# A slot list's compares, products and row normalisation are dealt out anew between VectorE, GpSimd and ScalarE

## The reference

```python
def _moe_forward(x, gate_w, wg, wu, wd):            # E = 8 experts, I = 512, K = 2
    x_flat = x.reshape(-1, h)
    logits = x_flat @ gate_w.T
    top_v, top_i = jax.lax.top_k(logits, K)
    probs = jax.nn.softmax(top_v.astype(jnp.float32), axis=-1).astype(logits.dtype)
    one_hot = jax.nn.one_hot(top_i, E, dtype=probs.dtype)
    combine = jnp.einsum('tk,tke->et', probs, one_hot)
    def body(acc, ws):
        wge, wue, wde, we = ws
        hidden = jax.nn.silu(x_flat @ wge.T) * (x_flat @ wue.T)
        return (acc + we[:, None] * (hidden @ wde.T), None)
...
x = L0_attn_x
x = x + 0.5 * _L0_ffn_ref(_layernorm(x, axis=-1), gate_w, wg, wu, wd)
x = x + _L0_attn_ref(_layernorm(x, axis=-1), ...)      # two mamba layers, one on the flipped sequence
x = x + 0.5 * _L0_ffn_ref(_layernorm(x, axis=-1), gate_w, wg, wu, wd)
```

## Time and profile before

| what | before |
|---|---|
| time, median of 3 runs | 2839.34 us (2837.99 to 2840.05) |
| the profiled execution: its own time, its span | 2840.15 us, 2838.0 us |
| first routing: normalised rows and logits up to the end of `choose(3)` | up to 51.49 us |
| first routing: the 16 batches, from the first `is_col` to VectorE's start on the lists | 62.22 to 104.96 us |
| second routing: end of `choose(3)`; the 16 batches | 2262.69 us; 2273.44 to 2316.2 us |
| busy shares over the span | PE 81%, DVE 81%, POOL 78%, ACT 67% |

### The profile page before, as it was taken

The page is one execution under the profiler, slowest core; times in us unless marked ns, Lnnn a source line. Parts: engine busy times, 40 slices in busy tenths (PEclk is TensorE's granted clock), DMA queues, the critical chain, the costliest instruction groups (busy, mean ns, idle before and its releaser), DMA issues.

```text
span 2838.0 us, 49251 instructions
## 1 busy us (share of the span) xinstructions
PE 2304.0 (81%) x15924; PEld 1961.5 (69%) x15924; DVE 2287.4 (81%) x3442; ACT 1909.5 (67%) x3640; POOL 2212.1 (78%) x1410
## 2 busy tenths in 40 slices
PE   4888888867887888988888888889897678888883
PEld 3778788835766766777676767677776467778772
DVE  8755555579999999999999999999999775555556
ACT  3344444448978979899999999999988434444441
POOL 3666666628989989999999999999999556666662
PEclk8999999988999999999999999999999889999996
DMA  7011111143333333333333333333333401111116
GB/s 229 20 40 41 40 41 41 39 142 94 103 96 96 101 93 104 104 101 111 102 109 106 108 106 103 106 106 104 110 103 109 160 12 41 41 40 41 40 40 192
DMA packets 155518, 249.13 MB, mean 88 GB/s; under 512 B 22194, under 2 KB 64082, under 8 KB 154578
## 3 DMA queue, kind: packets, MB, share of 16 engines
q1 hardware_dynamic: 136450, 202.92, 23.8%
q0 software_dynamic: 18464, 37.79, 5.0%
q10 hardware_dynamic: 432, 6.29, 0.6%
HBM read 213.36 MB, written 33.55 MB: 87 GB/s over the span
## 4 chain that ended last, share of the span: by engine, by line
PE 42%; DVE 16%; issue 15%; POOL 11%; ACT 10%; DMA 3%; another core or an unknown queue 3%; ACTq 0%; SPq 0%; POOLq 0%; DVEq 0%
PE bank L1339 13%; PE bank L1360 9%; POOL buf L544 8%; PE bank L1535 6%; DVE buf L909 5%; PE bank L1410 4%; PE bank L1510 3%; ACT over L1154 3%; PE bank L1320 3%; DVE X L796 2%; ACT scaled L1187 2%; DMA buf<-state_rows 2%; DVE buf L896 2%; POOL buf L531 2%
## 5 line engine op out<-in xcount | busy, mean ns | idle before, releaser
L544 POOL TENSOR_TENSOR buf<-buf 128x1024 f32<-128x1024 f32 x512 | 1200.6, 2380 | 68.3 <-PE bank L1535 40.1
L909 DVE TENSOR_TENSOR_SCAN buf<-over,bank 128x512 f32<-128x512 f32 x832 | 953.7, 1200 | 8.3 <-ACT over L1154 5.4
L1339 PE MATMUL bank<-parts 128*128 128x256 f32 x3456 | 530.3, 299 | 76.4 <-issue 73.7
L1154 ACT ACTIVATE over<-wgu,negA 128x510 f32<-128x510 f32 x832 | 541.4, 710 | 60.7 <-DVE buf L909 59.7
L1339 PEld LDWEIGHTS bank<-parts 128*128 128x128 f32 x3456 | 460.8, 198 | 96.9 <-issue 91.8
L1535 PE MATMUL bank<-id_sb,buf 128*128 128x128 f32 x4096 | 514.5, 279 | 6.7 <-POOL buf L544 6.7
L1535 PEld LDWEIGHTS bank<-id_sb,buf 128*128 128x128 f32 x4096 | 477.3, 144 | 57.0 <-issue 46.0
L493 POOL DMA_INDIRECT token_outputs<-buf,slot_out x288 | 298.3, 1036 | 266.8 <-ACT buf L1055 199.2
L768 DVE TENSOR_TENSOR buf<-buf,bank 128x512 f32<-128x512 f32 x288 | 196.8, 684 | 332.2 <-ACT buf L1049 204.1
L1187 ACT ACTIVATE scaled<-wd_sb,I 128x256 f32<-128x256 f32 x896 | 377.3, 497 | 22.0 <-PE bank L1510 21.9
L483 POOL DMA_INDIRECT buf<-token_rows,slot_token x288 | 298.9, 1038 | 96.7 <-issue 90.7
(11 more groups left out here) (169 smaller groups left out, 3003.7 us busy)
## 6 DMA issues: line engine op xcount, KB each, us to landing
buf<-state_rows SPq DMA_DIRECT2D x608, 256.0 KB, 3.3
token_rows<-buf SPq DMA_DIRECT2D x32, 256.0 KB, 2.3
wd_sb<-token_outputs SPq DMA_DIRECT2D x16, 512.0 KB, 4.5
buf<-token_outputs SPq DMA_DIRECT2D x16, 512.0 KB, 4.8
buf<-token_rows,slot_token POOLq DMA_INDIRECT x288
token_outputs<-buf,slot_out POOLq DMA_INDIRECT x288
out<-X SPq DMA_DIRECT2D x16, 256.0 KB, 3.6
wgu<-wgT ACTq DMA_DIRECT2D x1, 2048.0 KB, 8.3
```

The lines of the kernel that those rows point to most:

```text
L544: pool.tensor_tensor(hC[:, b, :].rearrange("p (c w) -> p c w", c=C), hs[:, b, :].rearrange("p (c w) -> p c w", c=C), Cs[:, b, :].unsqueeze ...
L909: V.tensor_tensor_scan(hs[:, b, w], dA[:, b, c, :, :].rearrange("p s t -> p (s t)"), source, 0.0, ALU.mult, ALU.add).then_inc(s[f"scan_don ...
L1154: ins = A.activation(dA[:, n % R, c, :, 1:], delta[r][:, c * W:(c + 1) * W].rearrange("p (s t) -> p s t", s=S)[:, :, 1:], ACT.Exp, scale=n ...
L1339: ins = M.matmul(bk[:, c * TP:(c + 1) * TP], w[:, b, cols], xx[:, b, :], start=(j == 0), stop=(j == 2))
```

## The change

Three numbers move, and one new piece of work is written for ScalarE.

- `ACT_TILES` is 3: ScalarE normalises three tiles of each group, VectorE one.
- `POOL_B` is 5: GpSimd multiplies five columns of a batch, ScalarE three.
- `PART_B` is 6: VectorE compares six of the eight partitions of a batch. ScalarE makes the other two as relu(1 - |lane - partition|): an `Abs` for each column with the partition as a bias, and, behind a wait for the two, one `Relu` over both. `hot_act` is therefore counted up twice in a batch, once behind the three products and once behind the `Relu`.
- VectorE copies the row of numbers from PSUM to SBUF once in each routing (`lanes`), since ScalarE reads it from there.

```diff
-ACT_TILES = 2
+ACT_TILES = 3
...
-        COLS, NB, POOL_B = TILES * HT, 8, 6
+        COLS, NB, POOL_B, PART_B = TILES * HT, 8, 5, 6
...
+        lanes = carve(10896, P)
...
                 def constants():
                     dve.wait_ge(s["iota_done"], m + 1)
+                    chain(V.tensor_copy(lanes, iota[:, 0:P]))
...
-                chain(V.tensor_copy(part_of, SLp))
+                chain(V.tensor_copy(part_of, SLp), "parts_known", m + 1)
...
-                    wait(dve, s["hot_act"], m * NBATCH + k - 1)
+                    wait(dve, s["hot_act"], 2 * (m * NBATCH + k - 1))
...
-                    V.tensor_tensor(hot_part[:, k % 2, :, :], iota[:, 0:P].unsqueeze(1).broadcast_to([P, NB, P]),
-                                    part_of[:, js].unsqueeze(2).broadcast_to([P, NB, P]),
+                    mine = slice(k * NB, k * NB + PART_B)
+                    V.tensor_tensor(hot_part[:, k % 2, 0:PART_B, :],
+                                    iota[:, 0:P].unsqueeze(1).broadcast_to([P, PART_B, P]),
+                                    part_of[:, mine].unsqueeze(2).broadcast_to([P, PART_B, P]),
                                     ALU.is_equal).then_inc(s["hot_part"], 1)
...
                     ins.then_inc(s["hot_act"], 1)
+                    act.wait_ge(s["parts_known"], m + 1)
+                    for j in range(PART_B, NB):
+                        at = k * NB + j
+                        ins = A.activation(hot_part[:, k % 2, j, :], lanes, ACT.Abs, scale=-1.0,
+                                           bias=part_of[:, at:at + 1])
+                    ins.then_inc(s["hot_apart"], 1)
+                    act.wait_ge(s["hot_apart"], m * NBATCH + k + 1)
+                    A.activation(hot_part[:, k % 2, PART_B:, :], hot_part[:, k % 2, PART_B:, :], ACT.Relu, scale=-1.0,
+                                 bias=1.0).then_inc(s["hot_act"], 1)
...
-                    pe.wait_ge(s["hot_act"], m * NBATCH + k + 1)
+                    pe.wait_ge(s["hot_act"], 2 * (m * NBATCH + k + 1))
```

More of the change, by code:

```diff
@@ L306, in macaron_kernel @@
             hot_pe hot_part is_col hot_pool hot_act ids_ready
-            gate_spread shift_all_done xn_act lT_pe lT_act lback_pe stats_done dve_norm act_norm xt_pre rstd_done xn_done moment before_done xt_done xnT_done
+            gate_spread shift_all_done xn_act lT_pe lT_act lback_pe stats_done dve_norm act_norm xt_pre rstd_done xn_done moment parts_known hot_apart before_done xt_done xnT_done
             logit_done logits_act route_dve route_pe route_act xin0 xin1 xin2
```

## The result

The changed kernel takes 2846.23 us (median of 8 runs, 2843.63 to 2849.77), the kernel before 2839.89 in the same comparison (2837.99 to 2841.57). The ratio is 1.002, with a 95% interval of 1.001 to 1.0029: slower by 6.3 us, with 2.8 to 8.2 us inside the interval. The forecast was 2843.0, with a range of 2837.5 to 2849.

The account below looks back on a forecast made before the run. VectorE was taken as the limit in both stretches, ScalarE 1.0 and 0.6 us ahead at the logits, TensorE close behind in the batches. Tiles +7.4 and batches -3.7 took 2839.34 to 2843.0 us, range 2837.5 to 2849.

Parts of the forecast that it names:

- the count of 12 tiles: Normalising part: extra ScalarE tiles of groups 4 to 15, 0.39 us each, 4.6 us ahead of quarter 2's logits copy.
- The sum: Both routings: +7.4 us from the tiles and -3.7 from the batches make +3.7 us.
- the loop: Batches: ScalarE and TensorE wait for each other over two batches, 4.40 us a turn, 2.20 a batch instead of 2.40.
- the two hand-overs: Batches: the passing between ScalarE and TensorE in one turn of the loop, taken as 0.11 us.
- the floor: Batches: VectorE's own pace with 256 fewer elements to compare, 2.14 us a batch.
- 0.75 us that is lost beside the steady batches: Ahead of the steady batches: TensorE starts 0.36 us later and batch 2 is filled 0.4 later, in each routing.
- The dear case: Rival: ScalarE's batch instructions cost more, the loop is 2.34 us, in all +8.0 us, 2847.3; chance 0.14.
- The cheap case: Rival: ScalarE's batch chain is 1.84 us, VectorE's 2.14 stays the pace, in all +1.6 us, 2840.9; chance 0.14.
- the logits are not on the path: Rival at `choose(2)`: the third tile delays logits by less than VectorE's lead, -5.9 us, 2833.4; chance 0.07.
- A clock that falls in the logits part: Rival: TensorE's spaced-out matmuls there drop to half clock, +19 us and more, 2862; chance 0.04.
- the forecast's own narrow range: Whole kernel: 2840 to 2846 us, from 0.36 to 0.41 us a tile and batch parts each a little off.

Follow-up runs that it names:

- e1: The kernel before with ACT_TILES = 3 and nothing else of the change: 2689.2 us against 2682.06, ratio 1.0026.
- e4: The changed kernel again without an edit, for a second trace: 2688.91 us against 2682.06 for the kernel before, ratio 1.002.
- e9: The changed kernel with added TensorE matmuls whose results nobody reads, ahead of logits and batches: 2842.2 us against 2840.41 for the kernel before, ratio 1.0005.
- the first trace: The profiled execution of the changed kernel without an edit, from the first comparison; its own time is 2846.79 us.
- e2: The changed kernel with ACT_TILES back at 2, the batches' part alone: 2682.67 us against 2682.06 for the kernel before, ratio 1.0001.
- e3: As e2, with ScalarE's third product back on GpSimd (POOL_B 6): 2679.52 us against 2682.06 for the kernel before, ratio 0.9989.
- e5: As e2, with a third buffer for hot_part and hot_col: 2672.68 us against 2679.83 for the kernel before, ratio 0.9972.
- e8: The kernel before again without an edit, one execution for a second trace; its own time is 2677.25 us.
- e10: The kernel before with a third tile on ScalarE in groups 0 to 3 only: 2841.73 us against 2840.41, ratio 1.0003.
- e11: As e6, with three compares on ScalarE and five on VectorE: 2833.04 us against 2840.41 for the kernel before, ratio 0.9977.
- e6: As e3, with three buffers for hot_part and hot_col: 2670.05 us against 2679.83 for the kernel before, ratio 0.9967.
- e7: The kernel before with three buffers for hot_part and hot_col and nothing of the change: 2675.96 us against 2679.83, ratio 0.9988.

## Why the prediction was right, point by point

**The tiles.** Right in place, mechanism and nearly in size. In the first routing the four traces with the third tile in every group end the last `choose` 3.2 (e1), 3.3 (e4, e9) and 4.2 us (the first trace) after the kernel before; 3.5 was forecast. In the second routing, counted from the constants that VectorE makes behind the `lanes` copy to the last `choose`, so that the projection ahead is left out, all nine traces without the tiles in the late groups have 37.2 or 37.3 us (before, e2, e3, e5 to e8, e10, e11) and the four with them 40.2 to 41.2: +3.0 to +3.9, forecast 3.9. e1 shows that this alone makes the change slower, e10 that the count of 12 tiles was right. The sum had taken TensorE's clock as in the trace of before; where it rises later, the term is 0.9 us larger. The wait ahead of `choose(0)`, which the forecast lacked, is harmless: VectorE waits again, and longer, ahead of `choose(2)`.

**The batches.** The step that was off is the loop: "One turn of that loop is 2.09 + 2.20 + 0.11 for the two hand-overs = 4.40 us". ScalarE's chain is 2.06, so that term was right, `Abs` at 386 ns and `Relu` at 417 with it:

```profile
L1033 ACT ACTIVATE buf<-buf x64: 384/386/388, 68.7 to 2320.1; 128x128 f32<-128x128 f32 x64
...
L1037 ACT ACTIVATE buf<-buf x32: 416/417/417, 69.4 to 2320.5; 128x256 f32<-128x256 f32 x32
```

TensorE's 2.20 was right as well. What was too small is the last term, 0.11 for the two hand-overs: they take 0.14 and 0.10 (the rows at 101.03 to 103.46 above). So the turn is 4.49 us and not 4.40. 13 steady batches gain 13 x 0.15 = 1.95 instead of 2.6, and the 16 together 1.2 in the first trace (0.5 to 1.3 in all six sets of e2, e4 and the first trace). The two sets that gain only 0.5 are those in which TensorE's granted clock comes back 9.4 us behind the first `is_col`; in the other four it is 7.5 to 8.3. e3, e5 and e6 show that the loop is the cause: a shorter chain or a third buffer brings most batches to VectorE's 2.13, which the forecast gave as the floor. e9 shows what the wait for the slow batch 0 costs ahead of the steady ones: 2.0 us of the 41.6. The kernel before has this wait too, and the forecast counted 0.75 us that is lost beside the steady batches; the traces have 0.8, as 0.4 up to batch 2's `hot_part` (7.8 instead of 7.4 us) and 0.4 behind the last `hot_part`, where the lists wait 4.6 instead of 4.2 us.

By the price list of the Trainium skill ("ScalarE: Activation LUTs", section "What ACT_TABLE_LOAD costs") the estimates are 386 ns for the `Abs` and 399 for the `Relu`. The first agrees with the measured 386; the `Relu` takes 417, and there the measurement decides.

**`lanes`.** Taken for hidden. In the first routing e2, e3, e5, e6 and e11 end their last `choose` 0.3 to 0.5 us after the kernel before, and in the second it stands on VectorE's path with its 0.3 in every trace that has it. Whether it is hidden in the changed kernel's first routing no run separates: e4, with it, ends 0.1 us after e1, without it, and the clock rises at different times in the two.

**The second routing's other 1.5 us.** Of the 5.8 us that it lost in the first trace, 3.9 is the tiles. The other 1.8 lies between the last gate and VectorE's constants, 9.8 us instead of 8.0; 0.3 of it is the `lanes` copy. TensorE's first 8 matmuls behind the last gate, and the window around them (columns as under e9, the granted clock is the third from the end), before:

```profile
2218.25 1.09 PE L1435 MATMUL bank<-id_sb,buf 128*128 128x128 f32 x8 [1.38 <-DVE buf L869]
```

```profile
2217.00:2219.00 2.00, 0.75 (x7) 0.75 (x8) 1.91 (x5) 0.06 (x1) 1.91 (x6) 1.00 0.00 0
```

and in the changed kernel:

```profile
2220.89 1.97 PE L1448 MATMUL bank<-id_sb,buf 128*128 128x128 f32 x8 [1.38 <-DVE buf L873]
```

```profile
2220.00:2222.00 2.00, 1.11 (x5) 1.11 (x6) 1.91 (x8) 0.00 (x0) 1.80 (x7) 0.50 0.00 0
```

The stretch takes 8.0 to 8.3 us in six traces (before, e4 to e8) and 9.3 to 10.0 in seven (after, e1, e2, e3, e9, e10, e11), with and without each part of the change, the changed kernel itself once in each set. In the six short ones the granted clock is 1.00 in the two microseconds behind the start of the last gate, in the seven long ones it stands at or falls to 0.50 there. So it is TensorE's clock in the one execution, and not fixed by the change. Whether the change shifts how often it is late is open: three of four traces with the third tile in every group have the long stretch, and four of nine without.

**The rivals.** The dear case was priced at 2847.3 and the time is 2846.23, so it names the time better than the forecast does, but not by its mechanism: the instructions cost what was forecast, the gap is the batches' 0.7 us a routing and the clock. The cheap case falls with the chain of 2.06 and the loop of 4.49. That the logits are not on the path is refuted by e1. A clock that falls in the logits part did not come: the window of 30 to 47 us has TensorE busy 15.19 of 17.00 with a granted clock of 1.00, the level of 2.4 GHz.

```profile
30.00:47.00 17.00, 15.19 (x68) 8.01 (x68) 10.04 (x33) 17.00 (x44) 4.33 (x8) 1.00 0.52 149
```

In the same row ScalarE is busy 17.00 of 17.00.

**The sum.** Forecast +3.7, measured +6.3 by medians and +6.8 by the traces. The 3.1 between are 1.4 from the batches, 0.7 from the first `choose` and 1.9 from the second, of which 1.5 is the clock, less 0.8 that the middle and the end of this trace were shorter. The direction and the mechanism were right; the forecast's own narrow range, 2840 to 2846, was just missed, and the terms that were off nearly all erred to the same side. That the total was off by 3 and not 4 us is luck: nothing in the change makes the middle and the end shorter.

## What to carry to other kernels

An engine that shows little busy time over the whole kernel can be full in the stretch to which work is moved: count its lead in that stretch (here 1.0 us against 12 tiles of 0.39) and not its share. With double buffers, the chain through two engines must fit into two periods, hand-overs included (here 0.24 us); moving work onto one of them can only gain until that loop closes. A third buffer for what the loop runs through, here 2176 columns of idle memory, took the redistributed batches from no gain that can be told (e2) to 7 us (e5), and was worth 4 us in the kernel before, with nothing moved (e7). Where a fast engine must first wait for one batch at half clock, a deeper buffer also hides that: 1.3 us a routing in e7.

## What was not expected of the hardware

- TensorE's clock rises at different points of the same program: near 23.9 and near 26.5 us in two executions of the changed kernel, and the stretch ahead of the second routing's constants takes 8 or 9.5 us by it. A trace pair that differs by 2 us in such a place is no evidence for an edit.
- The kernel before took 2682 and 2680 us on two chips and 2840 on a third. In the two traces of the changed kernel the first gate in the middle stage, whose first start the row of that line gives, comes at 613.3 (e4, first row) and at 689.5 us (first trace, second row), while the first routing ends within 0.3 us of the same time; so about half of the 160 us lies between the first routing and the middle stage, where the first experts' loop is. The other half lies behind the second routing, 442.5 and 521.4 us. Why was not tried.

```profile
L873 DVE TENSOR_TENSOR buf<-bank,wgu x64: 662/681/692, 613.3 to 2140.9; 128x512 f32<-128x512 f32 x64
```

```profile
L873 DVE TENSOR_TENSOR buf<-bank,wgu x64: 661/682/692, 689.5 to 2220.2; 128x512 f32<-128x512 f32 x64
```
